# Third layer's attention: the output product inside the attention loop instead of a phase behind it

## The chip, the cores and the metric

The kernel runs on one NeuronCore of a Trainium2 chip. The metric is the device time of one launch in microseconds (us). Five engines with queues of their own take part: TensorE (PE in the profile, its weight loads PEld), VectorE (DVE), ScalarE (ACT), GpSimd (POOL) and SyncE (SP), which only issues transfers.

## The reference

A residual network of four layers on x of (4, 1024, 128), float32. Every layer is `x = x + attention(layernorm(x)) + ffn(layernorm(x))`, with other formulas in each layer. The change concerns the third layer's attention, with 16 heads of width 8:

```python
q, k, v = (x @ Wq, x @ Wk, x @ Wv)          # each to (B, 16, T, 8)
attn = einsum('bhqd,bhkd->bhqk', q, k) / sqrt(8) + slopes * (arange(T) - 255)
probs = softmax(where(causal, attn, min), axis=-1)
out = einsum('bhqk,bhkd->bhqd', probs, v).transpose(0, 2, 1, 3).reshape(B, T, C)
return out @ Wo
```

The last line is what is moved. Its result is added to the residual x; the expert ffn of the same layer is added to x too, by gathering transfers that run during this attention.

## The kernel before, in words

`build` runs phases one behind the other, each an object of the class Phase with its own SBUF and PSUM tiles and semaphores; `Phase.end` is a barrier of all engines. In the third layer they are: `layernorm`, `front` (router, experts, q, k, v), `alibi_attention` (tiles a_...), `alibi_out` (tiles a2o_...), and behind it the fourth layer's `layernorm` and `wkv`.

`alibi_attention` (L810 to L1148) makes 16 iterations, four for each batch; an iteration is four heads ("units", HU = 4) over all 1024 tokens. It has ten steps (n = 0 to 9), for which the lists `sunits` and `eunits` name blocks of the score matrix.

- `first` (L975, matmuls of L986) computes scores of a later iteration ("ahead": five steps and one iteration), so that the maximum of each row is known early. Per step there are four units; the first two are issued at the step's start, the other two behind the masked scores. `maximum` on VectorE (L1106, L1108) reads them.
- `second` (L997, matmuls of L1006 and L1012) computes the scores again, with the maximum taken off and the mask; `exponentials` on ScalarE (L1073) reads the two PSUM tiles pE in turn and writes the weights to SBUF, two calls a step (in step 9 with only 512 elements a partition each).
- `weigh` (L1016, L1024) multiplies the step before's weights with V into pO; ScalarE copies pO to SBUF (`empty`, L1079) twice an iteration. `turn_out` (L1028, L1033) transposes that copy at steps 6 and 2, and `normalise` on VectorE (L1124, L1126) divides by the sum and writes the mix to the big tile XR.

All that VectorE reads goes through a **ring** of three PSUM tiles, pS. `take` numbers the uses in the order in which TensorE fills them: "s" a unit of scores, "m" the transposed maxima (L994, L1118), "o" a transposed output. Use number `at` lies in tile at % 3 and may be filled when VectorE has counted the semaphore `ring_out` past the use three before it:

```python
if lo == 0:
    pe.wait_ge(ring_out, at + half + 1)
ins = pe.matmul(pS[(at + half) % SB][:, lo:lo + n], ...
```

So the order of the work is written out by hand, the same for all engines. GpSimd splits each iteration's maxima into three bfloat16 rows (L923 to L930), which SyncE copies into the stacks, and then issues two of the 32 gathering transfers that add the experts' result to X (L935).

`alibi_out` (L1151 to L1211) works on eight chunks of 512 tokens (half a batch): VectorE gathers the mix of four iterations (L1200), TensorE transposes it (L1170), ScalarE copies the transposed tile to SBUF (L1192), TensorE multiplies with Wo (L1182), VectorE adds to X (L1210). Both PSUM tiles are double; VectorE first waits for all 32 gathering transfers.

## Time and profile before

| | us |
|---|---|
| median of 3 runs | 2445.22 |
| lowest, highest | 2440.64, 2445.56 |
| profiled execution | 2447.45 |
| its span | 2445.7 |
| PE busy | 2184.2 (89%) |
| DVE busy | 1706.7 (70%) |
| ACT busy | 1279.9 (52%) |
| POOL busy | 943.2 (39%) |

The page's busy times are of the whole span and mix the phases; the rows below are of the third layer's attention (1565 to 2034 us) and of the output phase behind it. In the timeline's rows of several instructions, the time is from the first one's start to the last one's end. Brackets at the end of a row give the idle time before it and what ended it. TensorE's ends are modelled and overlap the next start by some hundredths. PEclk is the granted clock, 1.00 is 2.4 GHz and 0.50 is 1.2 GHz.

### The profile page before, as it was taken

How to read it: one execution, taken by the hardware profiler on the slowest of the kernel's cores; microseconds unless marked ns; L12 is line 12 of the kernel's file. 1: busy time of each engine (PE TensorE's matmuls, PEld its weight loads, DVE VectorE, ACT ScalarE, POOL GpSimd, SP SyncE). 2: the span in 40 equal slices, each digit the busy share in tenths (PEclk: the TensorE clock that was granted, in tenths of full speed). 3: DMA queues.
4: the chain of work that ended last, by engine and by line, in shares of the span. 5: the costliest groups of instructions: out<-in, count | busy, mean ns of one | idle time of the engine just before them, and what ended most of it. 6: DMA issues, size and time to landing. Idle time of an engine off the chain costs nothing. (4 is left out here: it accounts for less than half of the span.)

```text
span 2445.7 us, 51189 instructions
## 1 busy us (share of the span) xinstructions
PE 2184.2 (89%) x19252; PEld 1326.0 (54%) x19252; DVE 1706.7 (70%) x5121; ACT 1279.9 (52%) x2752; POOL 943.2 (39%) x1175
## 2 busy tenths in 40 slices
PE   5579999998999999999999798799999996898886
PEld 2446667995666666766666675433333333333333
DVE  7656665674666677666666545599998964598896
ACT  2236665564666666666666533156666674423322
POOL 2026665663667743555433214011111110044462
PEclk9679999998999999999999979689999998999998
DMA  6311111313011100000000007201111100000000
GB/s 170 113 47 36 32 33 51 86 36 139 19 34 17 35 5 2 19 2 19 2 2 2 2 28 228 63 21 43 45 36 36 39 21 36 0 1 0 9 9 17
DMA packets 77909, 93.77 MB, mean 38 GB/s; under 512 B 10145, under 2 KB 56242, under 8 KB 76002
## 3 DMA queue, kind: packets, MB, share of 16 engines
q1 hardware_dynamic: 64178, 77.23, 10.5%
q0 software_dynamic: 13488, 13.28, 2.7%
q8 instruction: 154, 2.52, 0.4%
q14 instruction: 89, 0.73, 0.1%
HBM read 54.55 MB, written 35.53 MB: 37 GB/s over the span
## 5 line engine op out<-in xcount | busy, mean ns | idle before, releaser
L1073 ACT ACTIVATE WA<-a_E 128x1024 f32<-128x1024 f32 (+1 forms) x320 | 283.0, 939 | 128.7 <-PE a_E L1006 70.5
L536 PE MATMUL a1b_S<-a1b_Kf,a1b_Qf 64*128 64x512 f32 (+3 forms) x1152 | 281.0, 514 | 1.6 <-DVE a1b_firstmax L741 1.4
L464 POOL TENSOR_SCALAR WA<-WA,a1b_rinv 128x1024 f32<-128x1024 f32 (+3 forms) x192 | 142.2, 752 | 264.8 <-DVE a1b_rinv L756 264.4
L986 PE MATMUL a_S<-a_KS,a_QS 54*128 54x512 bf16 (+3 forms) x768 | 202.0, 352 | 37.6 <-DVE a_mx L1108 26.9
L748 DVE COPY a1b_PT<-a1b_T 128x512 f32<-128x512 f32 (+6 forms) x336 | 145.5, 445 | 122.7 <-PE a1b_T L549 122.1
L674 ACT COPY a1b_PT<-a1b_T 128x512 f32<-128x512 f32 (+6 forms) x336 | 127.9, 395 | 160.5 <-PE a1b_T L549 157.0
L568 PE MATMUL a1b_O<-a1b_PT,WA 128*64 128x128 f32 x2976 | 210.8, 277 | 0.0
L568 PEld LDWEIGHTS a1b_O<-a1b_PT,WA 128*64 128x64 f32 x2976 | 187.8, 137 | 40.0 <-ACT WA L674 17.5
L464 POOL TENSOR_SCALAR XR<-XR,a1b_rinv 128x896 f32<-128x896 f32 (+5 forms) x192 | 141.3, 747 | 125.2 <-DVE a1b_rinv L756 125.1
L986 PEld LDWEIGHTS a_S<-a_KS,a_QS 54*128 54x128 bf16 x768 | 53.5, 94 | 204.5 <-DVE a_mx L1108 92.7
L1024 PE MATMUL a_O<-WA,V 128*9 128x512 f32 (+3 forms) x1536 | 159.7, 504 | 0.1
L1106 DVE TENSOR_REDUCE a_mx<-a_S 128x1 f32<-128x512 f32 x256 | 156.8, 681 | 1.7 <-PE a_S L986 1.7
L668 ACT ACTIVATE WA<-WA,a1b_nmax 128x1024 f32<-128x1024 f32 (+3 forms) x192 | 149.7, 783 | 2.3 <-DVE a1b_nmax L741 2.2
L668 ACT ACTIVATE XR<-XR,a1b_nmax 128x896 f32<-128x896 f32 (+5 forms) x192 | 149.1, 780 | 0.0
L536 PEld LDWEIGHTS a1b_S<-a1b_Kf,a1b_Qf 64*128 64x128 f32 x1152 | 123.3, 189 | 44.8 <-DVE a1b_firstmax L741 32.7
L924 POOL CAST a_mrow<-WA 32x128 bf16<-32x128 f32 x16 | 4.5, 281 | 363.4 <-DVE WA L1118 363.4
L2141 POOL TENSOR_TENSOR a_Ss<-a_Sf,a_Sb 128x1024 f32<-128x1024 f32 x32 | 69.4, 2167 | 180.6 <-DVE a_Sb L2506 174.2
L741 DVE CUSTOM_DVE_ANT_0 WA<-a1b_S,a1b_tb 128x512 f32<-128x512 f32 (+1 forms) x192 | 107.8, 587 | 28.5 <-PE a1b_S L536 27.3
L1108 DVE CUSTOM_DVE_ANT_0 a_masked<-a_S,a_maskq,a_mx 128x256 f32<-128x256 f32 (+3 forms) x256 | 123.0, 544 | 1.6 <-PE a_S L986 1.5
L1006 PE MATMUL a_E<-a_QS,a_KS 54*128 54x512 bf16 (+3 forms) x768 | 117.1, 333 | 4.2 <-ACT WA L1073 3.9
L1108 DVE CUSTOM_DVE_ANT_0 a_masked<-a_S,a_maskq 128x512 f32<-128x512 f32 (+3 forms) x256 | 108.9, 486 | 12.5 <-PE a_S L986 12.5
L549 PEld LDWEIGHTS a1b_T<-ident,XR 64*128 64x128 f32 x1728 | 72.8, 139 | 75.6 <-issue 66.1
(443 smaller groups left out, 5280.1 us busy)
## 6 DMA issues: line engine op xcount, KB each, us to landing
WA<-in_w SPq DMA_DIRECT2D x8, 1024.0 KB, 9.0
a_QS<-qstack SPq DMA_DIRECT2D x32, 216.0 KB
a_KS<-kstack SPq DMA_DIRECT2D x32, 216.0 KB
a1b_tb<-tab SPq DMA_DIRECT2D x12, 512.0 KB
qstack<-f_parts SPq DMA_DIRECT2D x24, 256.0 KB
kstack<-f_parts SPq DMA_DIRECT2D x24, 256.0 KB
f_slots<-f1r_zrows SPq DMA_DIRECT2D x9, 516.0 KB
f1t_xs<-f_slots SPq DMA_DIRECT2D x9, 516.0 KB, 7.2
```

The costliest lines, as they stand in the source:

```text
L464: pool.tensor_scalar(v, v, rinv[:, e, part, u:u + 1], 1.0, ALU.mult, ALU.mult).then_inc(n_sb, 1)
L536: pe.matmul(pS[k % NB][:, 0:hi - lo], Qf[half, s, i * P:(i + 1) * P], Kf[half, s, lo:hi], start=True, stop=True).then_inc(s_ps, 1)
L568: ins = pe.matmul(pO[half, at:at + P], V[p % 2][:, j, half], turned(step, u, c)[:, k * P:(k + 1) * P], start=(j == 0), stop=(j == i))
L668: act.activation(v, v, ACT.Exp, bias=nmax[:, e, part, u:u + 1], scale=-1.0, accum_out=rsum[:, e, part, u:u + 1]).then_inc(p_sb, 1)
L674: ins = act.copy(dst, src)
L748: ins = dve.tensor_copy(dst, src)
L986: ins = pe.matmul(pS[(at + half) % SB][:, lo:lo + n], QS[s][ROW[half], pair, i * P:(i + 1) * P], KS[s][ROW[half], pair, c * CH:c * CH + n] ...
L1006: ins = pe.matmul(pE[q % 2][:, half, lo:lo + n], KS[s][ROW[half], q % 2, j * P:(j + 1) * P], QS[s][ROW[half], q % 2, (c + 1) * CH - n:(c + ...
L1024: ins = pe.matmul(pO[32 * u:32 * u + 9, CH - n:CH], V9[:, it, u, j, :], PT[(2 * k + u // 2) % NP][:, u % 2, lo:lo + n], start=(j == 0), st ...
L1073: act.activation(PT[q % NP][:, :, 0:w], pE[q % 2][:, :, 0:w], ACT.Exp).then_inc(e_sb, 1)
L1106: ins = dve.tensor_reduce(before, pS[at % SB][:, lo:lo + n], AX.X, ALU.max)
L1108: ins = dve.tensor_tensor_reduce(out=masked[:, at % 2, lo:lo + n], in0=pS[at % SB][:, lo:lo + n], in1=maskq[:, CH - n:CH], scale=1.0, scal ...
```

## The change

`alibi_out` goes. `normalise` writes the mix in the layout of the batch (token tiles by 128 channels). For a half batch that is complete, four things are put into the attention: at step 8 of a batch's last iteration for its first half, and at step 3 of the next iteration for its second half, TensorE transposes (`turn_mix`, four transposes in a ring tile, use "t"); in the following step ScalarE copies it to SBUF between its two exponentials (`copy_mix`) and gives the tile back by a semaphore of its own, `turned`; at that step's end TensorE multiplies with Wo in another ring tile (`output`, use "y"), and VectorE adds it to X (`add`) and gives it back by `ring_out`. The last batch's second half is done behind the loop. `vectors` counts the uses that VectorE gives back, and `free` chooses the semaphore. The gathering transfers count a semaphore for each batch.

```diff
     NS = 3
-    mix = G["XR"][:, :, :].rearrange("p a b -> p (a b)").rearrange("p (i t c) -> p i t c", i=IT, t=TT)
+    mix = G["XR"]
     QS = [ph.sb(f"QS{s}", [P, HW, T], BF16) for s in range(NS)]
...
     OT = w2[:, CH:3 * CH].rearrange("p (c t) -> p c t", c=2)
+    mT = w2[:, 4 * CH:6 * CH].rearrange("p (c t) -> p c t", c=2)
     rinv = ph.sb("rinv", [P, 2, CT, HU])
...
     MAXIMA, OUT0, OUT1 = 5, 6, 2
+    MIX = ((8, 0), (3, 1))
     EQ = STEPS * 2
...
         ring[use] = len(ring)
+
+    def finished(it, n):
+
+        if it % HU == HU - 1 and n == MIX[0][0]:
+            return it // HU, 0
+        if it and it % HU == 0 and n == MIX[1][0]:
+            return it // HU - 1, 1
+        return None
 
...
                 take("o", it, 0)
+            if finished(it, n):
+                take("t", *finished(it, n))
+            if n and finished(it, n - 1):
+                take("y", *finished(it, n - 1))
     take("o", IT - 1, 1)
+    take("t", B - 1, 1)
+    take("y", B - 1, 1)
+    by_scalar = sorted(at for use, at in ring.items() if use[0] == "t")
+
+    def vectors(at):
+        return at - sum(k < at for k in by_scalar)
+
+    def free(pe, at):
+
+        if at - SB in by_scalar:
+            pe.wait_ge(turned, by_scalar.index(at - SB) + 1)
+        elif at >= SB:
+            pe.wait_ge(ring_out, vectors(at - SB) + 1)
 
...
                     pool.indirect_dma_start(out=G["X"][:, t, :], out_offset=None, in_=ybuf[:, :], in_offset=place,
-                                            compute_op=ALU.add).then_inc(R["gathered"], 16)
+                                            compute_op=ALU.add).then_inc(R["gathered"][t // TT], 16)
 
...
                         if lo == 0:
-                            pe.wait_ge(ring_out, at + half + 1)
+                            free(pe, at + half)
                         ins = pe.matmul(pS[(at + half) % SB][:, lo:lo + n], QS[s][ROW[half], pair, i * P:(i + 1) * P],
...
                 at = ring["m", it]
-                pe.wait_ge(ring_out, max(at, SB + ring["s", it, STEPS - 1, HU - 1]) + 1)
+                pe.wait_ge(ring_out, vectors(ring["s", it, STEPS - 1, HU - 1]) + 1)
+                free(pe, at)
                 pe.transpose(pS[at % SB][0:ROWS, 0:P], mx[:, it % NS, :, :, :].rearrange("p h w t -> p (h w t)"),
...
                 pe.wait_ge(o_sb, 2 * it + c + 1)
-                pe.wait_ge(ring_out, at + 1)
+                free(pe, at)
                 for t in range(CT):
                     ins = pe.transpose(pS[at % SB][:, t * P:(t + 1) * P], OT[:, c, t * P:(t + 1) * P], G["ident"][:, :])
+                ins.then_inc(ring_in, 1)
+
+            def turn_mix(b, h):
+                at = ring["t", b, h]
+                it = b * HU + HU - 1
+                pe.wait_ge(ring_out, vectors(ring["o", it, h]) + 1)
+                free(pe, at)
+                for j in range(CT):
+                    ins = pe.transpose(pS[at % SB][:, j * P:(j + 1) * P], mix[:, b * TT + h * CT + j, :], G["ident"][:, :])
+                ins.then_inc(ring_in, 1)
+
+            def output(b, h):
+                at = ring["y", b, h]
+                pe.wait_ge(turned, 2 * b + h + 1)
+                free(pe, at)
+                for j in range(CT):
+                    ins = pe.matmul(pS[at % SB][:, j * P:(j + 1) * P], mT[:, h, j * P:(j + 1) * P], wo, start=True, stop=True)
                 ins.then_inc(ring_in, 1)
...
                         turn_out(it, 0)
+                    if finished(it, n):
+                        turn_mix(*finished(it, n))
+                    if n and finished(it, n - 1):
+                        output(*finished(it, n - 1))
             weigh(IT - 1, STEPS - 1)
             turn_out(IT - 1, 1)
+            turn_mix(B - 1, 1)
+            output(B - 1, 1)
 
...
                 act.copy(OT[:, c, :], pO[:, :]).then_inc(o_sb, 1)
+
+            def copy_mix(b, h):
+                if b:
+                    act.wait_ge(ring_in, ring["y", b - 1, h] + 1)
+                at = ring["t", b, h]
+                act.wait_ge(ring_in, at + 1)
+                act.copy(mT[:, h, :], pS[at % SB][:, :]).then_inc(turned, 1)
 
...
                     exponentials(it, 2 * n)
+                    if n and finished(it, n - 1):
+                        copy_mix(*finished(it, n - 1))
                     exponentials(it, 2 * n + 1)
             empty(IT - 1, 1)
+            copy_mix(B - 1, 1)
 
...
                     dve.wait_ge(ring_in, at + 1)
-                    if at >= 2:
-                        dve.wait_ge(ring_out, SB + at - 1)
+                    if vectors(at) >= 2:
+                        dve.wait_ge(ring_out, vectors(at) - 1)
                     for i, c, lo, n in keys(k):
...
                         else:
-                            ins = dve.tensor_tensor_reduce(out=masked[:, at % 2, lo:lo + n], in0=pS[at % SB][:, lo:lo + n],
+                            ins = dve.tensor_tensor_reduce(out=masked[:, vectors(at) % 2, lo:lo + n], in0=pS[at % SB][:, lo:lo + n],
                                                            in1=maskq[:, CH - n:CH], scale=1.0, scalar=before if c else -3.0e38,
...
                 dve.wait_ge(r_inv, 2 * it + c + 1)
-                dve.tensor_tensor(mix[:, it, c * CT:(c + 1) * CT, :].rearrange("p t (u d) -> p t u d", u=HU), v[:, :, :, 0:8],
+                b, g = divmod(it, HU)
+                rows = mix[:, b * TT + c * CT:b * TT + (c + 1) * CT, g * HU * 8:(g + 1) * HU * 8]
+                dve.tensor_tensor(rows.rearrange("p t (u d) -> p t u d", u=HU), v[:, :, :, 0:8],
                                   rinv[:, c, :, :].unsqueeze(3).to_broadcast([P, CT, HU, 8]), ALU.mult).then_inc(ring_out, 1)
 
-            dve.sem_inc(ring_out, SB)
+            def add(b, h):
+                at = ring["y", b, h]
+                dve.wait_ge(ring_in, at + 1)
+                dve.wait_ge(R["gathered"][b], 16 * TT)
+                c = b * TT + h * CT
+                xv = G["X"][:, c:c + CT, :]
+                dve.tensor_tensor(xv, xv, pS[at % SB][:, :].rearrange("p (k d) -> p k d", k=CT), ALU.add).then_inc(ring_out, 1)
+
             dve.wait_ge(consts, 6)
...
+            add(B - 1, 1)
 
 
-def alibi_out(nc, G, wo, R):
...
-                alibi_out(nc, G, w("L2o"), R)
...
-                R = dict(place=place, stores=3, stored=nc.alloc_semaphore("f2_stored"), gathered=nc.alloc_semaphore("f2_gathered"))
+                R = dict(place=place, stores=3, stored=nc.alloc_semaphore("f2_stored"), gathered=[nc.alloc_semaphore(f"f2_gathered{b}") for b in range(B)])
```

TensorE's queue around steps 8 and 9 of a batch's last iteration, before (L1024 weighing, L986 scores, L1006 and L1012 masked scores):

```order
L986 MATMUL a_S<-a_KS,a_QS 128x512 x2
L1006 MATMUL a_E<-a_QS,a_KS 128x256 x2
L1012 MATMUL a_E<-a_masks,a_units 128x64 x2
L1012 MATMUL a_E<-a_masks,a_units 128x128 x2
L1006 MATMUL a_E<-a_QS,a_KS 128x256 x2
L1012 MATMUL a_E<-a_masks,a_units 128x64 x2
L1012 MATMUL a_E<-a_masks,a_units 128x128 x2
L986 MATMUL a_S<-a_KS,a_QS 128x512 x2
L1024 MATMUL a_O<-WA,V 9x384 x4
L1024 MATMUL a_O<-WA,V 9x128 x4
L986 MATMUL a_S<-a_KS,a_QS 128x512 x2
```

and with the change, where these are L1053, L1014, L1035 and L1041:

```order
L1071 MATMUL a_S<-ident,XR 128x128 x4
L1014 MATMUL a_S<-a_KS,a_QS 128x512 x2
L1035 MATMUL a_E<-a_QS,a_KS 128x256 x2
L1041 MATMUL a_E<-a_masks,a_units 128x64 x2
L1041 MATMUL a_E<-a_masks,a_units 128x128 x2
L1035 MATMUL a_E<-a_QS,a_KS 128x256 x2
L1041 MATMUL a_E<-a_masks,a_units 128x64 x2
L1041 MATMUL a_E<-a_masks,a_units 128x128 x2
L1014 MATMUL a_S<-a_KS,a_QS 128x512 x2
L1053 MATMUL a_O<-WA,V 9x384 x4
L1053 MATMUL a_O<-WA,V 9x128 x4
L1079 MATMUL a_S<-WB,WA 128x128 x4
```

The transposes (L1071) stand between step 8's weighing and step 9's first two units of scores, the product (L1079) between step 9's weighing and the next step's scores; the second L1014 row holds the unit that takes the transposes' tile.

TensorE's queue at steps 3 and 4 of the following iteration, before:

```order
L1024 MATMUL a_O<-WA,V 9x256 x4
L986 MATMUL a_S<-a_KS,a_QS 128x512 x2
L1006 MATMUL a_E<-a_QS,a_KS 128x512 x4
L986 MATMUL a_S<-a_KS,a_QS 128x512 x2
L1024 MATMUL a_O<-WA,V 9x512 x4
```

and now:

```order
L1053 MATMUL a_O<-WA,V 9x256 x4
L1071 MATMUL a_S<-ident,XR 128x128 x4
L1014 MATMUL a_S<-a_KS,a_QS 128x512 x2
L1035 MATMUL a_E<-a_QS,a_KS 128x512 x4
L1014 MATMUL a_S<-a_KS,a_QS 128x512 x2
L1053 MATMUL a_O<-WA,V 9x512 x4
L1079 MATMUL a_S<-WB,WA 128x128 x4
L1014 MATMUL a_S<-a_KS,a_QS 128x512 x2
```

Here too the transposes (L1071) come ahead of a step's first scores and the product (L1079) behind its weighing; both are new in this queue.

ScalarE's queue from the copy of pO at step 4 to the next iteration's first steps, before (L1079 copies pO, L1073 are the exponentials):

```order
L1079 COPY WA<-a_O 128x512
L1073 ACTIVATE WA<-a_E 128x1024 x10
L1073 ACTIVATE WA<-a_E 128x2x256 x2
L1073 ACTIVATE WA<-a_E 128x1024 x2
L1079 COPY WA<-a_O 128x512
```

and now (L1131, L1125), with the copy L1138 of the transposed mix:

```order
L1131 COPY WA<-a_O 128x512
L1125 ACTIVATE WA<-a_E 128x1024 x10
L1125 ACTIVATE WA<-a_E 128x2x256
L1138 COPY WA<-a_S 128x512
L1125 ACTIVATE WA<-a_E 128x2x256
L1125 ACTIVATE WA<-a_E 128x1024 x2
L1131 COPY WA<-a_O 128x512
```

The copy stands between the two exponentials of step 9, so the second of them is behind it.

## Rows read from the trace of the kernel before

**Rows 1.** Stretches; columns: us, PE, PEld, DVE, ACT, POOL busy, PEclk, DMA share, GB/s
```profile
1750.00:1800.00 50.00, 46.62 (x496) 17.38 (x499) 47.38 (x157) 35.45 (x43) 9.05 (x12) 1.00 0.17 43
2000.00:2034.00 34.00, 28.63 (x333) 9.66 (x325) 2.48 (x9) 26.73 (x33) 4.52 (x6) 0.96 0.05 6
2034.00:2059.00 25.00, 15.67 (x96) 13.97 (x96) 8.26 (x16) 4.59 (x8) 0.00 (x0) 0.80 0.00 0
```

**Rows 2.** Timeline (start, us, engine line op out<-in, count), both ends of the output phase
```profile
2033.52 0.29 DVE L1126 TENSOR_TENSOR XR<-a_S,a_rinv 128x128 f32<-128x128 f32 x1
...
2058.34 0.69 DVE L1210 TENSOR_TENSOR X<-X,a2o_Y 128x512 f32<-128x512 f32 x1 [0.25 <-PE a2o_Y L1182]
```

**Rows 3.** Timeline, chunks of the output phase: one product at half clock, a chunk at full
```profile
2044.54 1.92 PE L1182 MATMUL a2o_Y<-WB,a2o_mT 128*128 128x128 f32 x8
...
2050.39 0.63 PE L1170 MATMUL a2o_T<-ident,a2o_rows 128*128 128x128 f32 x4 [1.21 <-DVE a2o_rows L1200]
...
2050.85 1.06 PE L1182 MATMUL a2o_Y<-WB,a2o_mT 128*128 128x128 f32 x8
2051.05 0.59 ACT L1192 COPY a2o_mT<-a2o_T 128x512 f32<-128x512 f32 x1 [2.14 <-PE a2o_T L1170]
```

**Rows 4.** Waits from 1700 to 1950: engine line <- waited for, us, times, longest
```profile
PEld a_S L986 <- DVE a_mx L1108: 47.3, 100, 0.9
...
DVE a_rinv L1124 <- PE a_S L1033: 6.5, 9, 0.7
```

**Rows 5.** Timeline, steps 8 and 9 of an iteration and the next one's first
```profile
1789.19 9.81 DVE L1106 TENSOR_REDUCE a_mx<-a_S 128x1 f32<-128x512 f32 x16
...
1791.23 0.39 PE L986 MATMUL a_S<-a_KS,a_QS 54*128 54x512 bf16 x2
...
1792.72 1.05 PE L1024 MATMUL a_O<-WA,V 128*9 128x384 f32 x16
1793.70 0.39 PE L986 MATMUL a_S<-a_KS,a_QS 54*128 54x512 bf16 x2
...
1791.86 1.09 ACT L1073 ACTIVATE WA<-a_E 128x512 f32<-128x512 f32 x2 [0.46 <-PE a_E L1012]
```

**Rows 6.** Timeline, steps 3 and 4 of the same iteration
```profile
1777.54 0.39 PE L986 MATMUL a_S<-a_KS,a_QS 54*128 54x512 bf16 x1 [0.36 <-DVE a_mx L1108]
...
1779.34 1.05 PE L1024 MATMUL a_O<-WA,V 128*9 128x512 f32 x8
...
1778.21 0.08 DVE L1108 DVE_READ_ACCUMULATOR2_ANT a_mx<- 128x1 f32 x1
...
1780.90 0.69 DVE L1108 CUSTOM_DVE_ANT_0 a_masked<-a_S,a_maskq 128x512 f32<-128x512 f32 x1
...
1778.18 1.94 ACT L1073 ACTIVATE WA<-a_E 128x1024 f32<-128x1024 f32 x2 [0.67 <-PE a_E L1006]
```

**Rows 7.** Timeline, the attention's last steps
```profile
2026.18 4.97 ACT L1073 ACTIVATE WA<-a_E 128x1024 f32<-128x1024 f32 x6 [0.56 <-PE a_E L1012]
...
2029.65 0.28 PE L1006 MATMUL a_E<-a_QS,a_KS 54*128 54x256 bf16 x2
...
2030.31 1.51 PE L1024 MATMUL a_O<-WA,V 128*9 128x384 f32 x24
...
2031.89 0.59 ACT L1079 COPY WA<-a_O 128x512 f32<-128x512 f32 x1 [0.74 <-PE a_O L1024]
```

**Rows 8.** Timeline of VectorE's reciprocals at step 2, and two stretches (columns of rows 1)
```profile
1718.56 0.26 DVE L1124 RECIPROCAL a_rinv<-a_S 128x16 f32<-128x16 f32 x1 [0.73 <-PE a_S L1033]
1747.61 0.26 DVE L1124 RECIPROCAL a_rinv<-a_S 128x16 f32<-128x16 f32 x1 [0.73 <-PE a_S L1033]
1774.48 0.26 DVE L1124 RECIPROCAL a_rinv<-a_S 128x16 f32<-128x16 f32 x1 [0.72 <-PE a_S L1033]
...
1719.00:1722.50 3.50, 2.67 (x23) 0.70 (x19) 3.50 (x18) 2.73 (x4) 0.00 (x0) 1.00 0.00 0
1723.00:1729.00 6.00, 5.90 (x25) 0.88 (x25) 4.65 (x16) 3.14 (x4) 0.00 (x0) 0.50 0.00 0
```

More of the change, by code:

```diff
@@ L807, in attention, with alibi_attention @@
     ph.end()
-def alibi_attention(nc, G, V9, qstack, kstack, w1, w2, ybuf, R):
+def alibi_attention(nc, G, V9, qstack, kstack, w1, w2, ybuf, wo, R):
     ph = Phase(nc, "a2")
@@ L855, in alibi_attention @@
     ring_in, ring_out, m_part, m_row = (ph.sem(n) for n in ("ringin", "ringout", "mpart", "mrow"))
-    e_ps, e_sb, weighed, o_sb, r_inv = (ph.sem(n) for n in ("eps", "esb", "weighed", "osb", "rinvs"))
+    e_ps, e_sb, weighed, o_sb, r_inv, turned = (
+        ph.sem(n) for n in ("eps", "esb", "weighed", "osb", "rinvs", "turned"))
     def ahead(it, n):
@@ L922, in _ @@
             for it in range(IT):
-                pool.wait_ge(ring_out, SB + ring["m", it] + 1)
+                pool.wait_ge(ring_out, vectors(ring["m", it]) + 1)
                 pool.tensor_copy(mrow[:, 0, :], minus).then_inc(m_part, 1)
@@ L1146, in _ @@
                         normalise(it, 0)
+                    if n and finished(it, n - 1):
+                        add(*finished(it, n - 1))
             normalise(IT - 1, 1)
-    ph.end()
-def alibi_out(nc, G, wo, R):
-    ph = Phase(nc, "a2o")
-    X = G["X"]
-    mix = G["XR"][:, :, :].rearrange("p a b -> p (a b)").rearrange("p (i t c) -> p i t c", i=4 * B, t=TT)
-    rows = ph.sb("rows", [P, 2, CT, 4, 32])
-    mT = ph.sb("mT", [P, 2, CH])
-    pT = [ph.ps(f"T{i}") for i in range(2)]
-    pY = [ph.ps(f"Y{i}") for i in range(2)]
-    r_sb, t_ps, t_sb, y_ps, y_sb = (ph.sem(n) for n in ("rsb", "tps", "tsb", "yps", "ysb"))
-    chunks = NT // CT
-    with nc.Block() as block:
-        @block.tensor
-        def _(pe):
-            def turn(c):
-                if c >= 2:
-                    pe.wait_ge(t_sb, c - 1)
-                pe.wait_ge(r_sb, c + 1)
-                for j in range(CT):
-                    ins = pe.transpose(pT[c % 2][:, j * P:(j + 1) * P],
-                                       rows[:, c % 2, j, :, :].rearrange("p g d -> p (g d)"), G["ident"][:, :])
-                ins.then_inc(t_ps, 1)
-            turn(0)
-            for c in range(chunks):
-                if c + 1 < chunks:
-                    turn(c + 1)
-                pe.wait_ge(t_sb, c + 1)
-                if c >= 2:
-                    pe.wait_ge(y_sb, c - 1)
-                for j in range(CT):
-                    ins = pe.matmul(pY[c % 2][:, j * P:(j + 1) * P], mT[:, c % 2, j * P:(j + 1) * P], wo,
-                                    start=True, stop=True)
-                ins.then_inc(y_ps, 1)
-        @block.scalar
-        def _(act):
-            for c in range(chunks):
-                act.wait_ge(t_ps, c + 1)
-                if c >= 2:
-                    act.wait_ge(y_ps, c - 1)
-                act.copy(mT[:, c % 2, :], pT[c % 2][:, :]).then_inc(t_sb, 1)
-        @block.vector
-        def _(dve):
-            def gather(c):
-                b, h = divmod(c, TT // CT)
-                if c >= 2:
-                    dve.wait_ge(t_ps, c - 1)
-                dve.tensor_copy(rows[:, c % 2, :, :, :].rearrange("p t g d -> p g t d"),
-                                mix[:, 4 * b:4 * b + 4, h * CT:(h + 1) * CT, :]).then_inc(r_sb, 1)
-            gather(0)
-            dve.wait_ge(R["gathered"], 16 * NT)
-            for c in range(chunks):
-                if c + 1 < chunks:
-                    gather(c + 1)
-                dve.wait_ge(y_ps, c + 1)
-                xv = X[:, c * CT:(c + 1) * CT, :]
-                dve.tensor_tensor(xv, xv, pY[c % 2][:, :].rearrange("p (k d) -> p k d", k=CT), ALU.add).then_inc(y_sb, 1)
```

2 lines of the change are left out of this document (1 added, 1 removed).

## The prediction

> **What bounds the kernel now.** I read first the stretch by stretch table [rows 1]. In the middle of the third layer's attention VectorE is busy 47.38 of 50 us and TensorE 46.62 (its ends are modelled, so it is less full than that), ScalarE 35.45. In the 25 us of the output phase nothing is full: TensorE 15.67, VectorE 8.26, ScalarE 4.59, TensorE at 0.80 of full clock. Then the order of time at both ends of that phase [rows 2]: the attention's last normalisation ends at 2033.81, the phase's last add at 2059.03. These 25.2 us are what can be won: a barrier, and then eight chunks that pass through transposes, ScalarE's copy, product and add with next to nothing beside them. A chunk's parts [rows 3] are, at full clock, 0.63, 0.59, 1.06 and (VectorE, [rows 2]) 0.69 us; at half clock the product takes 1.92.
>
> What the chunks will be put into is read from the waits in the attention [rows 4]. The score products of L986 wait for VectorE's maxima (100 times in 250 us, 47.3 us on this one line): they want a slot of the three-slot ring back. VectorE in its turn stands still only where a slot comes to it that isn't scores: before the reciprocal of L1124, 6.5 us in 9 waits, 0.73 us each. So VectorE sets the pace, at 26.87 us an iteration (reciprocal at 1747.61 to reciprocal at 1774.48, [rows 8]), with two or three slots of work ahead of it at the most, about 2 us. Whatever holds the ring longer than that, or takes VectorE's time, lengthens the program.
>
> **The change, part by part.**
>
> *Removed:* the phase. Its eight gathers of the mix on VectorE go altogether, since the normalisation now writes the batch's layout itself (same 128 elements a partition, 0.29 us as before [rows 2]; output runs of 32 instead of 128, for which the row with such runs, the gather, shows no extra cost; I take 0). The barrier between the phases goes as well. 25.2 us in all.
>
> *Left at the end:* the last half batch has nothing beside it: transposes 0.63, copy 0.59, product 1.06, add 0.69 [rows 2, 3], and four handovers of 0.05 (the copy starts at 2051.05, 0.03 after the transposes' end) make 3.15 us. At half clock the product alone would add 0.86.
>
> *The half batch before it* (batch 3, half 0) falls into the last iteration, where VectorE has nothing to do and ScalarE runs without a gap from 2026.18 to 2031.15 [rows 7]. The transposes push the last step's masked scores from 2029.65 to 2030.24, its first exponential from 2030.06 (2031.15 less 1.09 for the last two) to 2030.65; that takes 0.55, the copy 0.59, so the second exponential ends at 2032.34. The product can't start before the copy's end, 2031.84, and lets TensorE go at 2032.81; the last weighing follows (a third of the 1.51 us of its row) and the pO copy starts at 2033.4 instead of 2031.89: 1.5 us.
>
> *The six others* fall where VectorE sets the pace, three at steps 8 and 9, three at steps 3 and 4 of an iteration.
>
> Steps 8 and 9 [rows 5]: VectorE reduces 16 units from 1789.19 on, 0.613 us each, so the first of step 0 starts at 1794.09. Now TensorE puts the transposes between 1791.23 and 1791.83 (0.60: a row's end overlaps what follows, as the weighing's 1.05 from 1792.72 is followed at 1793.70, and in the same way the product holds TensorE for 0.97). Step 9's first two score units come at 1791.83 and are there at 1792.26, where VectorE was ready at 1791.63; it is through them at 1793.48. The third needs the transposes' slot, which ScalarE gives back. Its first exponential shifts from 1791.86 to 1792.46, takes 0.55 (half of 1.09), the copy ends at 1793.60, the scores are there at 1794.08: VectorE has stood another 0.6. The next two units last to 1795.30. Meanwhile TensorE weighs from 1793.88 to 1794.86 and multiplies to 1795.92; the add runs from 1795.96, and step 0's maxima start at 1796.57 instead of 1794.09. **2.5 us** a time, of which 0.61 is work of VectorE and the rest three waits.
>
> Steps 3 and 4 [rows 6]: the transposes fit in while TensorE would wait anyway. But step 4's second unit now wants the slot of step 3's last, read at 1778.29, so it goes from 1777.54 to 1778.35; the exponentials shift by the same 0.81, from 1778.18 to 1778.99; with 0.97 (half of 1.94) and the copy the slot is back at 1780.55 and the third unit is there at 1781.03, 1.47 us after VectorE was through with the second. Two units last to 1782.3. Weighing (1780.83) and product end at 1782.87, the add lets step 5 start at 1783.52 instead of 1780.90. **2.6 us**.
>
> Three of each: 15.3 us. Bounds: VectorE's own share alone, 6 x 0.61 = 3.7, if the waits vanished; and 6 x 3.1 = 18.6, if each handover (I took 0.05) cost 0.2 more at the three waits. The worked values lie nearest to what the reciprocal's wait shows (0.73 us for a slot filled by four transposes behind a weighing), and I take 15.3.
>
> *Waits that I cost at nothing:* the add now waits for its batch's eight gathers instead of all 32. GpSimd issues a pair behind each iteration's mask rows, which are made in the iteration before, so a batch's last pair is out more than 26.87 us before its first add. If one came late it would hold VectorE, behind it the ring, and so everything. The extra wait of the maxima's transposition is for a slot that was freed earlier. SyncE's loads and the mask rows keep their lead of most of an iteration. ScalarE's copies delay its later exponentials by 0.59; it is busy 35.45 of 50 us [rows 1] and catches up.
>
> *TensorE's clock.* Three times in this attention it falls to half (0.50, the 1.2 GHz level) for more than 6 us, behind 1722, 1859 and 1995, each time just after the steps 3 and 4 where TensorE waits for slots (busy 2.67 of 3.50 us ahead of it, [rows 8]). One such fall makes an iteration 29.05 us instead of 26.87: 2.2 us. In a chunk it also makes the product 0.86 longer, 3.0 together. The chunk at steps 3 and 4 adds about 1.4 us in which TensorE stands, that at steps 8 and 9 about 1.0. So more falls are likely, though they don't come each time: the same pattern of steps went by without one in four iterations of five. Bounds: no further fall, or one in each of the six chunks (18 us). I take one more than the three of before, 3.0 us, nearest to their rate (three in fourteen iterations, raised somewhat by the longer waits).
> The Trainium skill (TensorE: Matmul & The Clock Gate, "Part 4: PE-mode transpose" and "A second HAM failure mode: psum-queue depth-cycling") says that transposes don't count as activity for the gate, and that short idle times between groups of matmuls while PSUM slots are cycled can make the clock go back and forth. By that the 0.6 us of transposes would not shield a chunk, and it speaks for the rival below; the falls behind steps 3 and 4 agree with it, no row shows the part on transposes.
>
> **The sum.** 25.2 - 3.15 - 1.5 - 15.3 - 3.0 = 2.3 us won. The profiled execution took 2447.45 us, its span is 2445.7; the three runs shown have their median at 2445.22. From the median: 2443.0.
>
> **The rivals.**
> 1. *The chunks cost less.* If VectorE made the waits good, the price would be between its own work (3.7) and TensorE's (0.60 + 0.97 a chunk, 9.4 for six). Then 25.2 - 4.65 - 9.4 = 11.2 won: 2434. For it: TensorE isn't truly full. Against it: the ring is three slots deep, no lead is carried from one step to the next, and the reciprocal's waits show that VectorE does run dry. 0.15.
> 2. *The clock falls more often,* and the change is slower. Place: the chunks' waits for ScalarE's copy and for the product. Price 3.0 each. With no fall more the balance is 5.3 won, so it turns from two more on, and from four on it is slower by over 0.2% (4.9 us, about what a measurement of this kernel can tell from no change): 12 - 5.3 = 6.7 lost, 2452. For it: longer waits than those behind which it fell before, in six places. Against it: in the attention's last iteration TensorE idles about as often, and the clock stays at 0.96 [rows 1]. 0.18.
> 3. *ScalarE holds the slot longer than worked out,* for instance because its exponentials are late by a whole step: 3.5 us a chunk, 21 for six, 25.2 - 4.65 - 21 - 3 = 3.4 lost, 2448.6. 0.12.
> 4. The change doing something else than it says: the order shows eight transposes, copies, products and adds in their places, and no phase. 0.
>
> **Chances.** The forecast has 0.55, and its own range is 2438 to 2448 (no further fall to two, chunks at 2.2 to 2.9 us). Some 0.21 of it lies under 2440.3, so faster: 0.21 + 0.15 = 0.36. Slower than 2450.1: rival 2 and a little of rival 3, 0.20. Within 0.2%: 0.44. The range of 2433 to 2453 takes in rival 1 nearly down to its price, rival 3, and rival 2 with four falls; outside it are chunks at VectorE's own price and five falls or more.
>
> **What would show it.** After: the last add ends some 3 us behind the last normalisation. Before each of six adds VectorE waits about 0.6 us for the product, and about 0.6 or 1.5 us two units earlier for scores that waited for the copy. Iterations with a chunk are 2.5 us longer than 26.87, and those with two (4, 8 and 12 have the second half, 3, 7 and 11 the first) don't exist. The granted clock shows the falls: four would be as forecast, three would give 2440, seven 2452. It is wrong if VectorE's idle time in the attention rises by less than 8 or more than 18 us, or if the layer norm and the fourth layer behind it change by more than their shift.

## The result, and the profile after

| | before | changed |
|---|---|---|
| median, us | 2444.74 (10 runs) | 2438.65 (10 runs) |
| lowest, highest | 2440.64, 2446.07 | 2436.59, 2440.21 |
| profiled execution | 2447.45 | 2439.55 |
| its span | 2445.7 | 2437.7 |

The ratio is 0.9979, its 95% interval 0.9969 to 0.9989: 6.1 us by the medians, small, but the interval lies clear of 1. A second comparison, with the changed kernel built again, gave 2438.71 against 2444.02 (12 and 17 runs): 5.3 us.

Stretches of the changed kernel, columns as in [rows 1]:

```profile
1750.00:1800.00 50.00, 46.25 (x484) 16.91 (x478) 46.61 (x162) 34.00 (x41) 9.02 (x12) 1.00 0.15 36
2000.00:2048.00 48.00, 40.23 (x441) 15.35 (x441) 13.29 (x48) 35.18 (x44) 4.51 (x6) 1.00 0.03 4
```

The attention is as full as before, and the stretch behind it, in which TensorE was busy for 15.67 of 25 us, is gone. The end is now this (timeline of the changed kernel):

```profile
2043.19 0.66 PE L1062 MATMUL a_S<-ident,WA 128*128 128x128 f32 x4 [0.71 <-ACT WA L1131]
2043.89 0.26 DVE L1186 RECIPROCAL a_rinv<-a_S 128x16 f32<-128x16 f32 x1 [1.22 <-PE a_S L1062]
2044.18 0.29 DVE L1190 TENSOR_TENSOR XR<-a_S,a_rinv 128x128 f32<-128x128 f32 x1
2044.53 0.42 PEld L1071 LDWEIGHTS a_S<-ident,XR 128*128 128x128 f32 x4 [0.92 <-DVE XR L1190]
...
2045.27 0.59 ACT L1138 COPY WA<-a_S 128x512 f32<-128x512 f32 x1 [2.13 <-PE a_S L1071]
...
2047.11 0.69 DVE L1199 TENSOR_TENSOR X<-X,a_S 128x512 f32<-128x512 f32 x1 [2.64 <-PE a_S L1079]
```

From the last normalisation's end (2044.47) to the last add's end (2047.80) it takes 3.33 us; before, 25.22 [rows 2].

Now a half batch at steps 8 and 9, to be laid beside [rows 5]:

```profile
1709.01 0.66 PE L1071 MATMUL a_S<-ident,XR 128*128 128x128 f32 x4
1709.60 0.39 PE L1014 MATMUL a_S<-a_KS,a_QS 54*128 54x512 bf16 x2
...
1711.36 0.39 PE L1014 MATMUL a_S<-a_KS,a_QS 54*128 54x512 bf16 x2 [0.97 <-ACT WA L1138]
1711.68 1.05 PE L1053 MATMUL a_O<-WA,V 128*9 128x384 f32 x16
1712.66 1.16 PE L1079 MATMUL a_S<-WB,WA 128*128 128x128 f32 x8
...
1710.02 1.29 DVE L1168 TENSOR_REDUCE a_mx<-a_S 128x1 f32<-128x512 f32 x2 [0.57 <-PE a_S L1014]
1711.78 1.29 DVE L1168 TENSOR_REDUCE a_mx<-a_S 128x1 f32<-128x512 f32 x2 [0.47 <-PE a_S L1014]
1713.86 0.69 DVE L1199 TENSOR_TENSOR X<-X,a_S 128x512 f32<-128x512 f32 x1 [0.79 <-PE a_S L1079]
...
1710.72 0.58 ACT L1138 COPY WA<-a_S 128x512 f32<-128x512 f32 x1
```

Before, VectorE read 16 such units in one row of 9.81 us; now it stands three times, 0.57, 0.47 and 0.79 us. TensorE waits 0.97 us for ScalarE's copy, which is behind an exponential although the transposes ended at 1709.67. At steps 3 and 4, beside [rows 6]:

```profile
1725.54 0.39 PE L1014 MATMUL a_S<-a_KS,a_QS 54*128 54x512 bf16 x1 [0.42 <-DVE a_mx L1170]
...
1727.74 0.39 PE L1014 MATMUL a_S<-a_KS,a_QS 54*128 54x512 bf16 x2 [1.38 <-ACT WA L1138]
...
1728.16 0.75 DVE L1170 CUSTOM_DVE_ANT_0 a_masked<-a_S,a_maskq,a_mx 128x512 f32<-128x512 f32 x1 [1.33 <-PE a_S L1014]
...
1730.23 0.69 DVE L1199 TENSOR_TENSOR X<-X,a_S 128x512 f32<-128x512 f32 x1 [0.64 <-PE a_S L1079]
...
1726.18 1.02 ACT L1125 ACTIVATE WA<-a_E 128x1024 f32<-128x1024 f32 x1 [1.47 <-PE a_E L1035]
1727.10 0.58 ACT L1138 COPY WA<-a_S 128x512 f32<-128x512 f32 x1
```

The best ruler of the attention is VectorE's reciprocals, two an iteration (L1124 before, L1186 now). From the one at step 6 to the next at step 2 it is 15.40 us, and from there to step 6 another 11.46, to a hundredth, wherever nothing special lies between; only the last four, at the loop's end, are by themselves shorter (10.26, 12.34, 8.47 and 7.46). In the changed kernel the three intervals with steps 8 and 9 of a half batch are 17.95, 17.96 and 17.95, the three with steps 3 and 4 are 14.21, 14.20 and 14.22. **So a half batch costs 2.55 and 2.75 us, the six 15.9 us.**

The same intervals show what was not foreseen. Before, two of 11.46 are 13.65 and 13.67, and the one of 10.26 is 12.65: the clock is at half in them, and it fell each time about 4 us behind step 2's reciprocal, within step 4. Such a stretch is called a fall here. In the changed kernel's profile there is none: it has no stretch at half clock between 1611 and 2051 us.

The ledger, all from the two profiled executions, in us of the changed kernel against before:

| | |
|---|---|
| output phase, 25.22, replaced by 3.33 behind the attention | -21.9 |
| six half batches in the attention | +15.9 |
| the one in the last iteration (interval 9.13 for 7.45) | +1.7 |
| no fall of the clock (2.2, 2.2 and 2.4) | -6.8 |
| the interval after the third, 13.07, is 12.35 | -0.7 |
| attention's first reciprocal at 1623.12 for 1622.56 | +0.6 |
| barrier and layer norm behind the attention | +0.4 |
| fourth layer, starts of its first subtraction and of its last forward scan: 323.5 for 320.8 | +2.7 |
| sum (span: -8.0) | -8.1 |

The 0.7 isn't the clock's: the granted clock is 1.00 all through that interval, and one exponential of ScalarE starts 0.7 us late in it. The same 0.7 to 0.8 us stands there in the profiles of five of the thirteen executions (before, the delay without the work, the copy first again, both halves at steps 3 and 4, the product one step later), in the others it doesn't. What it waits for wasn't tried.

### The profile page after: what moved, and what is told of

The parts are those of the page before. It is cut to its first block and busy times, and to the rows that moved or that the text cites. A ratio compares the mean times of both kernels' runs of the same rounds, so it can differ in the third digit from the quotient of the medians.

```text
span 2437.7 us, 51184 instructions
## 1 busy us (share of the span) xinstructions
PE 2172.7 (89%) x19252; PEld 1322.8 (54%) x19252; DVE 1701.8 (70%) x5113; ACT 1278.1 (52%) x2752; POOL 939.7 (39%) x1175
## 5 line engine op out<-in xcount | busy, mean ns | idle before, releaser
L1125 ACT ACTIVATE WA<-a_E 128x1024 f32<-128x1024 f32 (+1 forms) x320 | 283.7, 940 | 135.1 <-PE a_E L1035 71.0
L1014 PE MATMUL a_S<-a_KS,a_QS 54*128 54x512 bf16 (+3 forms) x768 | 199.1, 349 | 45.7 <-DVE a_mx L1170 26.9
L1014 PEld LDWEIGHTS a_S<-a_KS,a_QS 54*128 54x128 bf16 x768 | 53.0, 94 | 203.8 <-DVE a_mx L1170 99.4
L1053 PE MATMUL a_O<-WA,V 128*9 128x512 f32 (+3 forms) x1536 | 154.9, 490 | 0.1
L1035 PE MATMUL a_E<-a_QS,a_KS 54*128 54x512 bf16 (+3 forms) x768 | 115.6, 328 | 3.8 <-ACT WA L1125 3.7
```

Source lines behind the costliest of these rows:

```text
L1014: ins = pe.matmul(pS[(at + half) % SB][:, lo:lo + n], QS[s][ROW[half], pair, i * P:(i + 1) * P], KS[s][ROW[half], pair, c * CH:c * CH + n] ...
L1035: ins = pe.matmul(pE[q % 2][:, half, lo:lo + n], KS[s][ROW[half], q % 2, j * P:(j + 1) * P], QS[s][ROW[half], q % 2, (c + 1) * CH - n:(c + ...
L1053: ins = pe.matmul(pO[32 * u:32 * u + 9, CH - n:CH], V9[:, it, u, j, :], PT[(2 * k + u // 2) % NP][:, u % 2, lo:lo + n], start=(j == 0), st ...
L1125: act.activation(PT[q % NP][:, :, 0:w], pE[q % 2][:, :, 0:w], ACT.Exp).then_inc(e_sb, 1)
```

## The experiments

The kernels were timed in five rounds beside the kernel before, but for the three further profiles, each of a single execution. Each comparison has its own median of the kernel before: 2444.02 for the changed kernel again, the copy first, the product ahead of the weighing and the product left out; 2445.84 for the others. `none` and `shift` leave the product with Wo out.

**The changed kernel again** (no edit).

> The changed kernel once more, to see whether the attention again runs without a stretch at half clock. Theory 1 (the six half batches shift the iterations against whatever makes the clock fall, so that the step pattern behind which it fell before is met less often): 0 or 1 falls in the attention, against 3 in the profile of before, and 2438 to 2440 us. Theory 2 (that there was none was luck of the one profiled execution): 2 to 4 falls, and a profile some 5 us longer than the first one's 2437.7. Either way the six intervals from reciprocal to reciprocal that hold a half batch are 17.96 and 14.20 us long, where no fall lies in them.

2438.71 us median of 12 runs (2433.93 to 2442.75), profile span 2440.2. The intervals with a half batch are 17.95, 17.94, 17.94 and 14.21, 14.21, and one of 15.77. The clock fell twice, once in step 4 of an ordinary iteration and once at the end of the first half batch at steps 3 and 4, while TensorE weighed and then multiplied with Wo (stretches of this kernel, columns as in [rows 1]):

```profile
1695.00:1702.00 7.00, 6.71 (x29) 1.05 (x30) 5.05 (x16) 3.54 (x4) 0.00 (x0) 0.51 0.00 0
1729.00:1732.00 3.00, 3.00 (x16) 1.50 (x15) 1.43 (x4) 0.53 (x1) 0.00 (x0) 0.54 0.00 0
```

The reciprocals around them, from its timeline:

```profile
1704.63 0.26 DVE L1186 RECIPROCAL a_rinv<-a_S 128x16 f32<-128x16 f32 x1 [0.90 <-PE a_S L1062]
1722.58 0.26 DVE L1186 RECIPROCAL a_rinv<-a_S 128x16 f32<-128x16 f32 x1 [0.73 <-PE a_S L1062]
1738.35 0.26 DVE L1186 RECIPROCAL a_rinv<-a_S 128x16 f32<-128x16 f32 x1 [0.90 <-PE a_S L1062]
```

The two cost 13.67 - 11.46 = 2.2 and 15.77 - 14.21 = 1.6. So neither expectation holds whole: the number of falls varies between executions of the same kernel, and was low in both.

**Further profiles of both kernels** (no edits).

> The kernel before, a second profile, for the clock. If the falls in the attention belong to its steps, there are again three, 136.5 us (five iterations and 2.2 us) apart and each behind steps 3 and 4, wherever the first one lies; if they are chance, their number and distance differ. The fourth layer, from its first subtraction to its last scan, took 320.8 us here and 323.5 in both profiles of the changed kernel: if that difference is the kernel's, it comes again.

> The kernel before, a third profile: the same as for the second, and the last scan again 320.8 us behind the fourth layer's start if that is the kernel's own, between 319.5 and 323.6 (the extremes of the other kernels) if it is the clock's.

> The changed kernel, a third profile. Its attention had no fall in one profile and two in the other. If its half batches keep the clock up, 0 to 2 again, none of them starting between the transposes and the product of a half batch's own steps but in the one case of the second profile; intervals of 17.95 and 14.21 us without a fall. The fourth layer's last scan at 323.5 us if that is the kernel's own.

| profile | falls in the attention | their cost, us | fourth layer, first subtraction to last forward scan, us | span, us |
|---|---|---|---|---|
| before | 3 | 6.8 | 320.8 | 2445.7 |
| before, 2nd | 3 | 6.8 | 322.6 | 2444.5 |
| before, 3rd | 3 | 6.6 | 319.5 | 2442.1 |
| changed | 0 | 0 | 323.5 | 2437.7 |
| changed, 2nd | 2 | 3.8 | 323.6 | 2440.2 |
| changed, 3rd | 0 | 0 | 323.6 | 2433.6 |

The kernel before has three falls in each profile, each in step 4, and from one to the next 136.5 us: five iterations of 26.87 and the 2.2 that a fall costs. Stretches of its second profile:

```profile
1723.50:1729.00 5.50, 5.31 (x25) 0.88 (x25) 4.45 (x15) 3.16 (x4) 0.00 (x0) 0.50 0.00 0
1860.00:1866.00 6.00, 5.77 (x25) 0.89 (x25) 4.77 (x16) 3.26 (x4) 0.00 (x0) 0.50 0.01 3
1996.50:2002.00 5.50, 5.26 (x22) 0.59 (x22) 2.19 (x8) 3.28 (x4) 0.00 (x0) 0.50 0.00 0
```

The changed kernel has 0, 2 and 0. On the mean of three profiles that is 5.5 us of the gain. The fourth layer, whose instructions are the same, gives part of it back: 323.6 against 321.0 on the mean. It varies between the profiles of before and not between those of the changed kernel, so neither expectation is settled by it.

Where the missing falls are missing matters for the cause. The three profiles of before have nine falls in 45 iterations. In the three of the changed kernel the nine iterations with a half batch at steps 3 and 4 have one, and the 36 others, whose own work is the same as before, have one too.

**The product left out.** Transposes, copy, product and add go, the waits for the gathering transfers stand at the attention's end:

```diff
-                    if finished(it, n):
-                        turn_mix(*finished(it, n))
-                    if n and finished(it, n - 1):
-                        output(*finished(it, n - 1))
...
-            add(B - 1, 1)
+            for b in range(B):
+                dve.wait_ge(R["gathered"][b], 16 * TT)
```

> Leaves the product with Wo out altogether (no transposes, copy, product or add, and no phase for it), so X lacks the third layer's attention. All intervals between reciprocals go back to 15.40 and 11.46 us. By the intervals of the changed kernel's profile its half batches cost 15.9 us (six), about 1.7 (the one in the last iteration) and 3.3 (the last), 20.9 in all. If the pattern of steps without half batches brings the three half-clock stretches of before back (7 us), the time is about 2425; if their number is chance, 2418 to 2425; if the half batches cost less than their intervals show, more than 2425.

2416.48 us (2415.17 to 2418.14), 22.2 less than the changed kernel beside it. All intervals are 15.40 and 11.46 again, the last four as given above, but for three of 13.68, 13.69 and 13.69: the falls are back, 136.6 us apart. The timeline of the reciprocals around the first (step 2, step 6, step 2):

```profile
1686.25 0.26 DVE L1171 RECIPROCAL a_rinv<-a_S 128x16 f32<-128x16 f32 x1 [0.73 <-PE a_S L1056]
1699.93 0.26 DVE L1171 RECIPROCAL a_rinv<-a_S 128x16 f32<-128x16 f32 x1 [0.90 <-PE a_S L1056]
1715.34 0.26 DVE L1171 RECIPROCAL a_rinv<-a_S 128x16 f32<-128x16 f32 x1 [0.73 <-PE a_S L1056]
```

Between the profiles (span 2413.5 for 2437.7) lie 24.2 us: 20.9 of half batches as worked out, less 6.7 for the falls, 6.0 because this attention's first reciprocal comes at 1617.12, and 4.0 in the fourth layer (319.5). The price by the intervals is the whole price; the median is lower than the 2425 that was expected with three falls, because the parts ahead and behind were quicker.

**The delay without the work.** As the last one, and in the six places VectorE reduces a constant tile four times:

```diff
+                    if n and finished(it, n - 1) and it < IT - 1:
+                        b, h = finished(it, n - 1)
+                        for k in range(4):
+                            dve.tensor_reduce(idle[:, 8 * b + 4 * h + k:8 * b + 4 * h + k + 1], maskq[:, :], AX.X, ALU.max)
```

> The kernel without the product (X lacks the third layer's attention), with nothing on TensorE or ScalarE in the six places, but four reductions of a constant tile on VectorE there, 4 x 0.61 = 2.45 us each: the delay of a half batch without its work. Intervals of 17.85 and 13.9 us. Theory 1 (the delays alone move the iterations against the clock's looks, and so the falls of before are missed): 0 or 1 falls in the attention and 2416.5 + 14.7 - 7 = 2424 us. Theory 2 (the transposes and products keep the clock up): three falls or more, since TensorE now stands still 2.4 us longer six times, and 2431 us or more.

2441.78 us (2436.36 to 2444.29), 4.1 below the kernel before beside it, where the kernel with nothing there was 27.5 below its own: 23.5 more, for 14.7 of delay. The changed kernel with all its work was 5.3 and 6.1 below. The intervals are 19.89, 19.07, 18.71 and 13.83, 15.02, 15.00 instead of 17.85 and 13.9. Nine stretches at half clock lie in this attention: three in ordinary iterations, as before (13.62, 13.60 and 12.60), five right behind a pause, and one that began 1.8 us ahead of a pause and cost nothing (the 13.83). The pause, in the timeline:

```profile
1710.90 2.46 DVE L1207 TENSOR_REDUCE a_idle<-a_maskq 128x1 f32<-128x512 f32 x4
```

The stretch around it and the one right behind it:

```profile
1709.00:1713.00 4.00, 2.59 (x33) 0.96 (x32) 4.00 (x8) 2.51 (x4) 0.00 (x0) 1.00 0.43 130
1713.50:1719.50 6.00, 5.49 (x45) 1.70 (x45) 4.82 (x8) 2.53 (x3) 0.00 (x0) 0.51 0.17 47
```

The same stretch of the changed kernel, with transposes and product in it:

```profile
1709.00:1713.00 4.00, 3.03 (x43) 1.69 (x40) 2.96 (x5) 1.76 (x4) 0.00 (x0) 1.00 0.24 62
```

Here the clock stays up behind it (it has no stretch at half clock, as said). With the pause TensorE is busy for 2.59 of 4 us, and then its clock is at half. Theory 1, that the delays alone remove falls, does not hold for this delay: none is removed, and five are added. The number of falls and the time are as theory 2 expected, but its cause isn't shown by that. The pause is one wait of 2.46 us, while a half batch's waits on VectorE are two or three of 0.5 to 1.3 us, so the shape of the wait differs as well as the work in it. Transposes and product were not put in alone. And work that stands in six places doesn't say by itself why the other 36 iterations have one fall for the nine in 45 of before.

**The copy first.** ScalarE copies the transposed mix ahead of both exponentials of its step:

```diff
-                    exponentials(it, 2 * n)
                     if n and finished(it, n - 1):
                         copy_mix(*finished(it, n - 1))
+                    exponentials(it, 2 * n)
                     exponentials(it, 2 * n + 1)
```

> Theory: two of the three waits in a half batch come from ScalarE giving the transposes' tile back late, behind an exponential that it need not wait for, since it is idle when the transposes end. With the copy ahead of both exponentials, step 9's third unit is no longer late (worked out: 17.96 becomes 17.3), nor is step 4's (14.20 becomes 12.8), 3 x (0.67 + 1.36) = 6 us less than the changed kernel, about 2432.5. Rival (the waits only show where VectorE stands, the cost is TensorE's extra work of 1.6 us a half batch): the intervals shorten by less than 1 us for the three pairs together, 2438.

> The kernel with the copy first once more, beside the two that are built on it: 2429.8 us again, intervals 17.36 and 12.68; one to three falls of the clock in the attention.

2429.84 us (2427.85 to 2430.78), ratio 0.9944 (0.9931 to 0.9957); beside the next kernels 2433.05 (2431.07 to 2438.25), ratio 0.9953 (0.9939 to 0.9966). Intervals 17.36 and 12.68 in both: a half batch costs 1.96 and 1.22 instead of 2.55 and 2.75, 6.4 us together, where 6 were worked out. The timeline of step 9 in this kernel:

```profile
1707.22 0.59 ACT L1138 COPY WA<-a_S 128x512 f32<-128x512 f32 x1 [0.52 <-PE a_S L1071]
1707.74 1.09 ACT L1125 ACTIVATE WA<-a_E 128x512 f32<-128x512 f32 x2
...
1707.54 2.48 DVE L1168 TENSOR_REDUCE a_mx<-a_S 128x1 f32<-128x512 f32 x4 [0.57 <-PE a_S L1014]
1710.79 0.69 DVE L1199 TENSOR_TENSOR X<-X,a_S 128x512 f32<-128x512 f32 x1 [0.76 <-PE a_S L1079]
```

The copy runs in ScalarE's idle time, the exponentials come no later, and VectorE's middle wait is gone; the two others, behind TensorE's own work, stay. Each of these two profiles has one fall, in an ordinary iteration, and the fourth layer takes 319.5 and 319.7, which is 4.1 and 3.9 less than in the changed kernel. By the profiles beside one another (spans 2426.9 and 2440.2) 6.4 us of the 13.3 are the intervals', 4.1 the fourth layer's, 1.6 the falls' (2.1 against 3.8) and 1.2 lie ahead of the attention; by the medians it is 8.9.

**The product ahead of the weighing,** on top of it:

```diff
+                    if n and finished(it, n - 1):
+                        output(*finished(it, n - 1))
                     if n:
                         weigh(it, n - 1)
...
-                    if n and finished(it, n - 1):
-                        output(*finished(it, n - 1))
```

> The copy first, and the product with Wo ahead of the weighing of the same step, right behind its last scores. Theory: what is left of a half batch's price, 1.3 to 1.8 us, is TensorE's own 1.6 us of transposes and product; the product's place only moves VectorE's wait from before the add to before the next step's scores. So the time is that of the kernel with the copy first, within 1 us (2432.5). Rival (the wait before the add is a price of its own, 0.64 to 0.79 us six times): another 3 to 4 us less, about 2429.

Intervals 17.42 and 12.81: within 0.13 of those without the edit, as the theory has it; the last iteration's half batch costs another 0.2. But the time is 2434.76 (2433.19 to 2436.77), 4.9 us more than the copy-first kernel beside it (whose repetition, put against its own kernel before, would make this 3.5). Its profile has four falls in the attention, none in a half batch's own interval (13.64, 12.59, 12.59 and 13.68 for 11.46: 6.7 us), where the copy-first kernel has one, and 321.5 for 319.5 in the fourth layer: of 8.2 us between the spans 4.5 are falls, 2.0 the fourth layer. An edit that costs some 0.8 us in its places goes with a time that is some 4 us longer; in these two profiles most of the difference is in where the clock falls.

**Both halves at steps 3 and 4,** in two iterations one behind the other, the copy first:

```diff
-        if it % HU == HU - 1 and n == MIX[0][0]:
-            return it // HU, 0
-        if it and it % HU == 0 and n == MIX[1][0]:
-            return it // HU - 1, 1
+        if it == IT - 1 and n == MIX[0][0]:
+            return B - 1, 0
+        if it >= HU and it % HU < 2 and n == MIX[1][0]:
+            return it // HU - 1, it % HU
```

> Copy first, and both halves of batches 0 to 2 at steps 3 and 4 (the first half in the iteration behind the batch, the second one iteration later); batch 3 as before. Theory: at steps 3 and 4 TensorE waits for VectorE anyway, so half of its extra work is free there and a half batch costs 1.22 us (12.68 against 11.46) instead of 1.96 (17.36 against 15.40) at steps 8 and 9: 3 x 0.74 = 2.2 us less than the kernel with the copy first, whose interval of 17.36 goes back to 15.40. Rival: the price is the same everywhere, VectorE's add and its wait for the product; then no interval changes in sum.

The intervals of 17.36 are 15.41 again, and the second half batch of each pair has 12.68: 3 x (1.96 - 1.22) = 2.2 us less, as worked out. But the first of each pair has 14.25, 14.24 and 14.25, with a fall in each, 1.57 above 12.68, and of the iterations behind the pairs two have 12.60 for 11.46 and one 11.54 for 10.26, with a fall each: six in this profile. Stretches of it, one behind the first pair and one in the second pair's first half batch:

```profile
1780.00:1785.00 5.00, 4.71 (x23) 0.89 (x26) 3.95 (x13) 2.70 (x3) 0.00 (x0) 0.66 0.01 3
1836.00:1838.00 2.00, 2.00 (x11) 0.13 (x8) 1.74 (x6) 1.87 (x2) 0.00 (x0) 0.50 0.04 8
```

So a half batch's work doesn't keep the clock up by itself: here three of six have a fall, which begins in step 4, behind the transposes and ahead of the product, 4.0 to 4.1 us behind step 2's reciprocal as in an ordinary iteration. The runs lie in two groups, 2429.35 and 2430.35, and 2436.6, 2437.18 and 2437.35, with a mean granted clock of 0.943 and 0.942 against 0.934, 0.936 and 0.930; the profiled one is of the upper. The median (2436.6, ratio 0.9948, 0.9935 to 0.9962) says nothing against the copy-first kernel beside it.

**The product one step later,** behind the first two units of step 5, on top of that. The ring's use "y" moves with it, and so does VectorE's add:

```diff
                 for u in range(HU):
+                    if u == 2 and n >= 2 and finished(it, n - 2):
+                        take("y", *finished(it, n - 2))
                     take("s", *ahead(it, n), u)
...
                         first(*ahead(it, n), 0)
+                        if n >= 2 and finished(it, n - 2):
+                            output(*finished(it, n - 2))
```

> As the kernel with all halves at steps 3 and 4, but the product and its add come one step later, behind the first two units of step 5's scores, so that VectorE has two units of work while TensorE multiplies. Theory: the wait of 0.64 us before the add goes, and a half batch costs little more than VectorE's add, 0.7 us instead of 1.22: 12.2 us intervals and 3 us less over six. Rival (as when the product was put ahead of the weighing, which changed no interval by more than 0.13): TensorE's work sets the price, 12.7 as before.

2427.52 us (2425.9 to 2435.39), ratio 0.9928 (0.9914 to 0.9942): the best median here, 18.3 below the kernel before. Intervals 12.38 to 12.40, so a half batch costs 0.93, between the two expectations (timeline of the first one):

```profile
1727.26 1.13 PE L1081 MATMUL a_S<-WB,WA 128*128 128x128 f32 x8 [0.37 <-DVE a_mx L1176]
...
1727.65 0.68 DVE L1176 CUSTOM_DVE_ANT_0 a_masked<-a_S,a_maskq 128x512 f32<-128x512 f32 x1
...
1728.43 0.69 DVE L1205 TENSOR_TENSOR X<-X,a_S 128x512 f32<-128x512 f32 x1
```

The add begins 0.10 us behind the last maximum: the wait for the product is gone. Of the 0.93 us 0.61 are the add. Again two groups: three runs from 2425.9 to 2427.52, two at 2433.3 and 2435.39, with 3 ordinary and 2 shorter falls in the profile of the latter, none in the six half batches' intervals. The mean granted clock doesn't tell these groups apart (0.934, 0.934 and 0.940 against 0.934 and 0.931).

## Why the prediction was right, and where it wasn't

2443.0 was forecast, 2438.65 measured, in the range and inside the forecast's own 2438 to 2448, near its edge. The steps:

- *What bounds it, and that the ring carries no lead:* right. The half batches' delays stay in the intervals to a hundredth and are never made good (rival 1 falls).
- *The phase* (25.2): right; *the last half batch* (3.15): 3.33, the weight loads of L1071 began 0.06 after the normalisation and the product's row is 1.16, not 1.06, long. *The half batch in the last iteration* (1.5): 1.7.
- *The six others* (15.3 by chains of 2.48 and 2.62): 15.9, by 2.55 and 2.75. The waits are where they were put: 0.57, 0.47 and 0.79 at steps 8 and 9 (worked out 0.63, 0.60 and 0.66), 1.33 and 0.64 at steps 3 and 4 (1.47 and 0.6). Rival 3 falls. That the copy's place behind an exponential makes two of the waits is shown by the copy-first kernel.
- *Waits costed at nothing:* right; no add waited for a gathering transfer (all of the 13.5 us before the eight adds are the product's).
- *TensorE's clock* is the step that failed, in sign. "I take one more than the three of before, 3.0 us": measured were 0, 2 and 0 falls against 3, 3 and 3, a gain of 5.5 us on the mean instead. I took TensorE's waits in a half batch as making falls likelier, by their length. The experiment with the delay alone shows that this can be so for one long wait (five falls behind six pauses), but in the changed kernel one fall lies in nine half batches at steps 3 and 4, none in nine at steps 8 and 9, and one in its 36 ordinary iterations. Why there are so few stays open: the half batches' own 1.8 us of matmuls may be part of it, but with both halves at steps 3 and 4 three of six half batches have a fall (in the other four profiles with the copy first none of 24). The price of a fall within a half batch was 1.6 us, not 3.0. The rule of the Trainium skill that spoke against the change (TensorE: Matmul & The Clock Gate, "Part 4: PE-mode transpose") isn't tested by that, as the product, which isn't a transpose, stands beside the transposes. Its other section, "A second HAM failure mode: psum-queue depth-cycling", agrees with the three falls in each profile of before.
- *The fourth layer* was taken to shift only. Its 323.6 us against 321.0 take back 2.6; in the other kernels the same instructions take 319.5 to 321.6. Why isn't shown. The amount of half clock doesn't order these times: the mean granted clock of that stretch is 0.95 in the three profiles of the changed kernel, and 0.92 in the profiles of before and of the product left out that took 319.5.

Two of the signs by which the prediction called itself wrong did come. VectorE's idle time in the attention (from 1565 to the last normalisation) rose from 65.4 to 71.1 us, by 5.7 where 8 was the least: the half batches' waits are there, but the idle time of three falls and the 0.7 are gone. And the fourth layer changed by 2.7 us beyond its shift.

So the error of 4.35 us in the total is in the main the clock's. Between forecast and profiles the clock in the attention makes 8.5 us (3.0 lost were forecast, 5.5 won on the mean); the fourth layer takes 2.6 of that back, and the half batches and the end another 1.0 (15.9 for 15.3, 1.7 for 1.5, 3.33 for 3.15). That leaves 4.9; the other 0.55 lies between profiles and medians, and in the starting value, 2445.22, which ten runs put at 2444.74. That the total still came out inside 2438 to 2448 was partly luck: with the clock's true share and all else as forecast it would have been 2434.5.

## What to carry to other kernels

- Work that moves into a loop paced by a short ring costs what it holds the ring, not what it is: here 0.61 us of VectorE's work cost 2.6. Ask for every use of the ring which engine gives it back, and what stands ahead of that on this engine's queue; moving one copy ahead of an exponential that it need not wait for won 6.4 of 15.9 us.
- Let the pacing engine have a unit of its own work while the other makes its product: 2.75, 1.22 and 0.93 us are the same half batch at steps 3 and 4, with the copy first, and with the product one step later. The place where TensorE waits anyway was the cheaper one (1.22 for 1.96) only once the copy no longer held the ring; before, it was the dearer (2.75 for 2.55).
- Where differences are below 10 us, lay a ruler of equal intervals along both traces before explaining a median. Here it separates the edit (to 0.01 us) from the falls of the clock, which cost 0 in two profiles of the changed kernel and 3.8 us in the third.

## What the runs showed of the hardware

- TensorE's clock falls in a regular beat with the program: in four profiles of two kernels without half batches three falls each, some 136.5 us apart, always in the same step, 4.0 to 4.2 us behind the same instruction, for 2.2 to 2.4 us each.
- Five and more runs of one kernel can lie in two groups 7 us apart (2429.35 and 2430.35 against 2436.6 to 2437.35), and of two kernels whose edit changes no ordinary or half batch interval by more than 0.13 us, but for the falls, one is 4.9 us slower in the same comparison.
- A delay on VectorE of 14.7 us in all cost 23.5. Of the 8.8 more, 6.3 lie in the intervals with the pauses, where TensorE, left without work, came back at half clock five times of six. With 1.8 us of TensorE's own work in the same places a fall lies in one of eighteen half batches of the changed kernel, in none of 24 of the kernels with the copy first (two profiles), with the product ahead of the weighing and with the product one step later, and in three of six with both halves at steps 3 and 4.
